# Separate rings for the B rows and the C rows of a selective scan, and dt's bias written into delta's buffer

## The reference, cut to what matters

```python
dlt, Bm, Cm = jnp.split(u @ W_x.T, [64, 80], axis=-1)      # 64 ranks, 16 B rows, 16 C rows
delta = jax.nn.softplus(dlt @ W_dt.T + b_dt)
A = -jnp.exp(A_log)                                        # 256 channels x 16 states
dA = jnp.exp(einsum('bld,dn->bldn', delta, A))
dBu = einsum('bld,bln,bld->bldn', delta, Bm, u)
# in chunks of 32 positions: carry = a * carry + bu ; y = sum over states of carry * C
y = y * silu(res);  out = y @ W_out.T + b_out
```

## Time and profile before

| | us |
|---|---|
| median of three runs | 1179.11 |
| lowest and highest run | 1177.35, 1183.39 |
| the profiled execution: its time | 1166.19 |
| the profiled execution: its span, first to last instruction | 1164.5 |
| busy in the span: PE, DVE, POOL, ACT | 1028.6, 785.3, 669.2, 650.5 |
| moved by DMA in the span | 176.69 MB |

### The profile page before, as it was taken

How to read it: one execution, slowest core, us unless ns; L and a number is a source line. 1 busy time by engine, 2 the same in 40 slices (tenths; PEclk the granted TensorE clock), 3 DMA queues, 4 the chain that set the end, 5 groups by cost and what they waited for, 6 DMA issues and landing times.

```text
span 1164.5 us, 12622 instructions
## 1 busy us (share of the span) xinstructions
PE 1028.6 (88%) x4164; PEld 556.4 (48%) x4164; DVE 785.3 (67%) x1564; ACT 650.5 (56%) x1021; POOL 669.2 (57%) x572
## 2 busy tenths in 40 slices
PE   5999999998999999779899998988997879776865
PEld 4986668553356455434445444533543324222441
DVE  3322415878667876887687777888789788878721
ACT  3235557576956768555556768466644644543211
POOL 2122236566766477656856567756856876865501
PEclk9989999999888999989899999889898999898976
DMA  4002003535444353555544434645464656566320
GB/s 117 10 1 82 1 27 131 216 144 187 137 160 164 110 208 110 179 201 182 217 154 160 176 120 170 242 164 204 160 250 161 233 203 242 197 207 242 109 82 10
DMA packets 55721, 176.69 MB, mean 152 GB/s; under 512 B 7332, under 2 KB 17896, under 8 KB 51560
## 3 DMA queue, kind: packets, MB, share of 16 engines
q1 hardware_dynamic: 55656, 175.89, 42.8%
HBM read 172.99 MB, written 2.88 MB: 151 GB/s over the span
## 4 chain that ended last, share of the span: by engine, by line
PE 50%; DVE 14%; POOL 13%; ACT 10%; issue 6%; DMA 4%; SPq 1%; POOLq 0%; DVEq 0%; ACTq 0%
PE yp L1464 11%; POOL dbu L654 5%; PE mp L1349 4%; PE mp L1339 4%; PE fp L1253 4%; PE fp L1247 4%; DMA bcast<-held 3%; PE fp L1232 3%; PE pp L1378 3%; DVE dA L949 3%; PE pp L1308 2%; PE pp L1313 2%; PE yp L1446 2%; ACT a_z L997 2%; ACT L980 2%
## 5 line engine op out<-in xcount | busy, mean ns | idle before, releaser
L654 POOL TENSOR_TENSOR dbu<-du,bcast 128x1024 f32<-128x1024 f32 x128 | 302.7, 2368 | 148.3 <-DMA bcast<-held 78.8
L1464 PE MATMUL yp<-hs,ident 128*128 128x512 f32 x512 | 276.3, 673 | 32.3 <-DVE hs L956 25.7
L949 DVE TENSOR_TENSOR_SCAN dA<-dA,dbu 128x512 f32<-128x512 f32 x192 | 226.3, 1215 | 66.1 <-ACT dA L1191 44.7
L1191 ACT ACTIVATE dA<-delta,mA 128x496 f32<-128x496 f32 x256 | 165.9, 669 | 133.0 <-DVE dA L959 101.6
L1464 PEld LDWEIGHTS yp<-hs,ident 128*128 128x128 f32 x512 | 103.2, 214 | 161.5 <-issue 109.3
L882 DVE SCALAR_TENSOR_TENSOR he<-mp,vectors,he 128x512 f32<-128x512 f32 x128 | 89.6, 742 | 50.7 <-PE mp L1339 35.9
L956 DVE TENSOR_TENSOR hs<-dA,bcast 128x1024 f32<-128x1024 f32 x96 | 117.5, 1224 | 4.2 <-PE yp L1464 1.1
L1339 PE MATMUL mp<-cont,w_e 64*128 64x512 f32 x256 | 92.3, 685 | 13.7 <-DVE he L882 12.1
L980 ACT ACT_TABLE_LOAD x76 | 97.5, 1283 | 1.4
L638 POOL TENSOR_TENSOR hs<-hs,bcast 128x1024 f32<-128x1024 f32 x32 | 77.1, 2409 | 33.9 <-DVE hs L949 33.7
L949 DVE TENSOR_TENSOR_SCAN hs<-dA,dbu 128x512 f32<-128x512 f32 x64 | 75.0, 1206 | 18.3 <-ACT dA L1191 17.4
(11 more groups left out here) (217 smaller groups left out, 1554.4 us busy)
## 6 DMA issues: line engine op xcount, KB each, us to landing
bcast<-held SPq DMA_DIRECT2D x128, 1024.0 KB, 5.5
he<-gates SPq DMA_DIRECT2D x32, 1024.0 KB, 7.9
xin<-L_attn_x SPq DMA_DIRECT2D x8, 256.0 KB, 4.4
out<-xo SPq DMA_DIRECT2D x8, 256.0 KB, 2.3
held<-bc SPq DMA_DIRECT2D x8, 64.0 KB, 2.1
he<-conv_wT SPq DMA_DIRECT2D x1, 384.0 KB
w<-w1T SPq DMA_DIRECT2D x1, 256.0 KB, 3.1
he<-w2T SPq DMA_DIRECT2D x1, 256.0 KB, 3.7
```

The costliest lines, as they stand in the source:

```text
L654: pool.tensor_tensor(out=dbu[:, j % 2, :].rearrange("p (r t) -> p r t", r=2), in0=d, in1=b_n, op=ALU.mult).then_inc(dbu_r.sem, 1)
L949: dve.tensor_tensor_scan(out=h, data0=dA[:, half], data1=dbu[:, j % 2, half], initial=0.0, op0=ALU.mult, op1=ALU.add).then_inc(hs_r.sem, 1)
L1191: act.activation(out=dst, in_=src, func=ACT.Exp, scale=mA[:, c, n:n + 1]).then_inc(dA_r.sem, 1)
L1464: last = pe.matmul(yp[:, :], lhsT=ident[:, :], rhs=hs[:, j % 2, r * SEQ:(r + 1) * SEQ], start=(k == 0 and r == 0), stop=(k == PAIRS - 1 an ...
```

## The change

1. `bcast` (three slots with B and C together, 24 KB in a partition) becomes `b_rows` with four slots and `c_rows` with three, 28 KB in a partition. Each has semaphores for its slots. SP has a thread for each (letters B and C), and issues two DMAs of 512 KB for a step where it issued one of 1 MB. A B slot waits only for the `dbu` of step j-4. A C slot waits only for the multiplication by C of step j-3. The multiplications by C now wait for their own rows.
2. ACT writes W_dt's product plus bias into `delta`'s buffer, and Abs and the last step of softplus read it there. The wait for POOL's gate work moves from this write to the next sequence's write of `res`.
3. `m_bin2`, a small tensor of the setup, lies in the experts' memory `he`.
4. The table `ORDER` is another on all five engines.

```diff
-SLOTS = 3
+B_SLOTS, C_SLOTS = 4, 3
...
-        dab, dtb = cv, res
+        dab = cv
...
-        bcast = sb("bcast", [P, SLOTS, 2, 2 * SEQ])
+        b_rows = sb("b_rows", [P, B_SLOTS, 2 * SEQ])
+        c_rows = sb("c_rows", [P, C_SLOTS, 2 * SEQ])
...
+        m_bin2 = he[0:2, 6, INNER:2 * INNER]
...
-                            if j >= SLOTS:
-                                sp.wait_ge(dbu_r.sem, j - SLOTS + 1)
-                                _, by_pool, by_dve = with_c(j - SLOTS)
-                                if by_pool:
-                                    sp.wait_ge(hc_pool, by_pool)
-                                sp.wait_ge(hc_dve, by_dve)
-                            src = held[i % 2, :, 2 * k:2 * k + 2, :].rearrange("(a s) r t -> a s (r t)", a=1)
-                            sp.dma_start(bcast[:, j % SLOTS, :, :], src.broadcast_to([P, 2, 2 * SEQ])
-                                         ).then_inc(bc_in[j % SLOTS], 16)
+                    for j in range(i * STEPS, (i + 1) * STEPS):
+                        yield True
+                        if j % STEPS == 0:
+                            sp.wait_ge(bc_out.sem, bc_out.at(i, 16))
+                        if j >= B_SLOTS:
+                            sp.wait_ge(dbu_r.sem, j - B_SLOTS + 1)
+                        sp.dma_start(b_rows[:, j % B_SLOTS, :], rows(i, 0, j % PAIRS)).then_inc(b_in[j % B_SLOTS], 16)
+
+            def spread_c():
+                for j in range(BATCH * STEPS):
+                    yield True
+                    if j % STEPS == 0:
+                        sp.wait_ge(bc_out.sem, bc_out.at(j // STEPS, 16))
+                    if j >= C_SLOTS:
+                        _, by_pool, by_dve = with_c(j - C_SLOTS)
+                        if by_pool:
+                            sp.wait_ge(hc_pool, by_pool)
+                        sp.wait_ge(hc_dve, by_dve)
+                    sp.dma_start(c_rows[:, j % C_SLOTS, :], rows(j // STEPS, 1, j % PAIRS)).then_inc(c_in[j % C_SLOTS], 16)
...
-                            pool.wait_ge(bc_in[j % SLOTS], 16 * (j // SLOTS + 1))
+                            pool.wait_ge(b_in[j % B_SLOTS], 16 * (j // B_SLOTS + 1))
...
-                                dve.tensor_tensor(out=hs[:, j % 2, :], in0=dA[:, :], in1=bcast[:, j % SLOTS, 1, :],
+                                dve.wait_ge(c_in[j % C_SLOTS], 16 * (j // C_SLOTS + 1))
+                                dve.tensor_tensor(out=hs[:, j % 2, :], in0=dA[:, :], in1=c_rows[:, j % C_SLOTS, :],
...
+                    if i >= 1 and c == 0:
+                        act.wait_ge(g4_r.sem, g4_r.at(i - 1, 1))
                     act.activation(out=res[:, c, :], in_=pp[:, :], func=ACT.Identity,
...
-                    if c == 0:
-                        act.wait_ge(g4_r.sem, g4_r.at(i, 1))
-                    act.activation(out=dtb[:, c, :], in_=pp[:, :], func=ACT.Identity,
+                    act.activation(out=delta[:, b, c, :], in_=pp[:, :], func=ACT.Identity,
...
     "SP":
-        "AGAGGBBBBABBBGBGGBBBBBBAGGGBBBBBBBBBBBGBGGBABBBGGGBBBBBBBBBDBABBGBGGBBBGBBBBBBBGGBBBBBGBGGBBDGABBBGG"
+        "AGAGGBCCCBBBBABBCBCBCCBBGCGBGCBCBCBGCGGBCBACCCBCBBBBCCBBCBCBCCBBCBCGBGGCCBBACBGCBCCCBBBBCBCGGBCBCBCB"
```

More of the change, by code:

```diff
@@ L42 @@
+        "CBBCDBCBCCBBGGGCBCBCCCDGGGD",
     "Pool":
[L43 to L46, removed]
+        "FFFFFFFFFAFAFFFFFBBAAFFFAFFAASSFSASFFSSSSSFFAFASSSBBSAFSAFSFSSSSASFAFSSSSFAFSSFSSASBABSSSFAFFASAFSFS"
@@ L47 @@
+        "SSSASSFASASFBFSBASSSSASSBFBAFFASSASFSAFSSSSSFAAFBFSBASSSBSFBSASSFSFASASASSSFSFSASSSSAFSAFSSBFSBASSAS"
+        "FSSFFSSBBSSAASASSFASSFSSBASBSSSFASASSSSBBSSAASSSASASSSSSASSASASBSBSASSSSSSSSABASBSSSSSASSASSSSABASSS"
+        "BSSSSSSSSSSSSSAABBBB",
     "DVE":
[L48 to L50 removed]
@@ L356, in build @@
         yg = sb("yg", [P, IC, SEQ])
-        bc_in = [sem(f"bc_in{k}") for k in range(SLOTS)]
+        b_in = [sem(f"b_in{k}") for k in range(B_SLOTS)]
+        c_in = [sem(f"c_in{k}") for k in range(C_SLOTS)]
         dA_r = signal("dA_r", 2 * STEPS)
@@ L426, in _ @@
             load(ld_mamba, m_edge[:, :], A["conv_wT"][0:2, :])
-            load(ld_mamba, m_bin2[:, :], row(A["L1_attn_b_in_row"][0:INNER]).broadcast_to([2, INNER]))
+            load(ld_mamba, m_bin2, row(A["L1_attn_b_in_row"][0:INNER]).broadcast_to([2, INNER]))
             load(ld_mamba, mw_x[:, :, :], A["mamba_W_xT"].rearrange("(c p) m -> p c m", p=P))
@@ L445, in spread @@
                     if i >= 2:
-                        for s in range(SLOTS):
-                            used = sum(j % SLOTS == s for j in range((i - 1) * STEPS))
-                            sp.wait_ge(bc_in[s], 16 * used)
+                        for arrived in (b_in, c_in):
+                            for s in range(len(arrived)):
+                                used = sum(j % len(arrived) == s for j in range((i - 1) * STEPS))
+                                sp.wait_ge(arrived[s], 16 * used)
@@ L467, in gating, with rows @@
+            def rows(i, which, k):
+                src = held[i % 2, which, 2 * k:2 * k + 2, :].rearrange("(a r) t -> a (r t)", a=1)
+                return src.broadcast_to([P, 2 * SEQ])
             def gating():
@@ L637, in times_c @@
                 h = hs[:, j % 2, :]
-                pool.tensor_tensor(out=h, in0=h, in1=bcast[:, j % SLOTS, 1, :], op=ALU.mult).then_inc(hc_pool, 1)
+                pool.wait_ge(c_in[j % C_SLOTS], 16 * (j // C_SLOTS + 1))
+                pool.tensor_tensor(out=h, in0=h, in1=c_rows[:, j % C_SLOTS, :], op=ALU.mult).then_inc(hc_pool, 1)
             def s_thread():
@@ L652, in s_thread @@
                             d = du[:, i % 2, c, :].rearrange("p (a t) -> p a t", a=1).broadcast_to([P, 2, SEQ])
-                            b_n = bcast[:, j % SLOTS, 0, :].rearrange("p (r t) -> p r t", r=2)
+                            b_n = b_rows[:, j % B_SLOTS, :].rearrange("p (r t) -> p r t", r=2)
                             pool.tensor_tensor(out=dbu[:, j % 2, :].rearrange("p (r t) -> p r t", r=2),
@@ L904, in before_scan @@
                 dve.wait_ge(mln_r.sem, mln_r.at(i, 1))
-                dve.scalar_tensor_tensor(out=delta[:, b, :, :], in0=dtb[:, :, :], scalar=0.0, in1=dab[:, :, :],
+                dve.scalar_tensor_tensor(out=delta[:, b, :, :], in0=delta[:, b, :, :], scalar=0.0, in1=dab[:, :, :],
                                          op0=ALU.max, op1=ALU.add).then_inc(delta_r.sem, 1)
@@ L1156, in before_scan @@
                 act.wait_ge(dtb_r.sem, dtb_r.at(i, IC))
-                ch.add(act.activation(out=dab[:, :, :], in_=dtb[:, :, :], func=ACT.Abs))
+                ch.add(act.activation(out=dab[:, :, :], in_=delta[:, b, :, :], func=ACT.Abs))
                 ch.wait()
```

59 lines of the change are left out of this document (28 added, 31 removed).

## The result

The changed kernel takes 1157.53 us as a median of four runs (1155.21 to 1160.93). The kernel before took 1181.25 us beside it (1177.35 to 1190.7). The ratio on record is 0.9873, 95% interval 0.9828 to 0.9919. A later set of six runs gave 0.9829 (0.9787 to 0.9871). So it is 1.3 to 1.7% faster; 1165 us had been forecast, a ratio of 0.988. The two medians of the first set stand 23.7 us apart, more than its ratio says. Those are four runs each; in the later sets, with over 20 runs of the kernel before, its median is 1175.3 to 1177.1 us, 18 to 20 us above the changed kernel's.

The account below looks back on a forecast made before the run. PE was taken to bound the scan before 880 us, a loop of waits through the copies after it. Gains of 12 + 3 + 1 less 2 made 14 us, so 1179.1 - 14 = 1165 us, range 1154 to 1173.

Parts of the forecast that it names:

- What bounds the late stretch: From 880 to 1100 us no engine is full; the path runs copy, `dbu`, scan, multiplication by C, next copy.
- B rows in four slots: 12 + 3 us: B copies issued about two steps earlier end POOL's copy waits: 12 us gained after 880 us, 3 before.
- rival A: Late stretch: the wait moves to DVE's loop and nothing is won; gain 2 us, 1177 us; chance 0.20.
- The order: -2 us: PE's last expert pieces move behind the scan: 2 us lost in the tail; moves at changes of sequence summed to nothing.
- C rows add no wait: C copies have until the multiplication three steps later, about 20 us at the mean step; costed at nothing.
- Twice as many copies: nothing: SP issues 128 more copies, 46 us, covered by its waits for the multiplications; costed at nothing.
- The landing of half a copy: Copies of 512 KB: 5.5 us taken for the later half, ends 0 and 7.9, all within the new lead.
- The bias: 1 us: Bias of dt written into delta's buffer no longer waits for POOL's gate work; 1 us gained of 0 to 4.7.
- B's mechanism: Rival: delta comes late at changes of sequence, the first scan waits for Ln through `dbu`; slower, 1187 us; chance 0.17.
- C's time: Rival: copies were on the path wherever the chain has them late; gain 28 us, 1151 us; chance 0.11.
- D: Rival: half copies hold the DMA engines as long as whole ones, 7.9 us a step; 1273 us; chance 0.02.
- The signs of being right: POOL's B-row wait under 10 us, DVE's late `dbu` wait near 5, scan 10 to 20 shorter, no C-row wait, copies off chain.

Follow-up runs that it names:

- e4: Kernel before, old order and ring, but from the fourth step on a copy brings only 64 of the 1024 elements of each row; ratio 0.9995.
- e12: Kernel before's order and bias of dt in res, with the separate rings of four B and three C slots; ratio 0.9960 to the kernel before.
- e11: Kernel before with its order and ring, only the bias of dt written into delta's buffer; ratio 0.9980.
- e1: Changed kernel's separate rings and bias of dt in delta's buffer, with the order of the kernel before; ratio 0.9926 to the kernel before.
- e13: The changed kernel run again, nothing changed; median 1157.20 us, ratio 0.9829 to the kernel before.
- e5: Changed kernel with copies of 64 of the 1024 elements of each row from a slot's second use on; median 1156.97 us, ratio 0.9825.
- e6: Changed kernel with three B slots and four C slots in place of four and three; ratio 1.0016 to the kernel before.
- e7: Changed kernel with three B slots and three C slots; ratio 1.0041 to the kernel before.
- e3: Changed kernel, but the B copy also waits for the multiplication by C of step j-3, so no early B; ratio 0.9993 to the kernel before.
- e2: Kernel before (one ring of three slots, whole copies, bias in res) with the changed kernel's order; ratio 1.0332 to the kernel before.
- e10: Kernel before's order, two copies for a step without early B, bias of dt in delta's buffer; ratio 0.9945 to the kernel before.
- e8: Changed kernel with the bias of dt written into res again; median 1164.55 us, ratio 0.9892 to the kernel before.

## Why the prediction came out right, and which terms were wrong

1. **What bounds the late stretch.** Right as a reading of the chain: the copies left it, and `dbu` with them. Wrong as a price list: in the old order e4 took more than half of the copy waits away and e12 nearly all, and the time fell by nothing that can be told (e4) and by 0.4% (e12).

2. **B rows in four slots: 12 + 3 us.** This is the term that was mis-sized. POOL's waits for copies did go, as I took them to (none in the changed kernel, 6.5 us in e12), but with the order held this brought 0.4% (e12), some 5 us, with an interval from 1 to 8. The sum had given it 15. One sentence that failed is "I take 4 us for all this" for what stands behind a waiting `dbu`: ScalarE's wait for POOL's layer norm steps did not move (71.0 us in e12, 70.5 before). The other is the 8.1 + 3 us of DVE's waits: they fell by 6.9, from 20.9 us over the whole span to 14.0 in e12, DVE's waits for exponentials stayed (44.7 before, 45.5 in e12), and the scan from first to last `dbu` is 2.0 us shorter in the one profiled execution, 8.0 us against e11's. POOL's waiting has moved from the copies to DVE's scans (68.4 before, 100.4 in e12), so for the most part it waited for copies in time that it had to spare. That is rival A, for the greater part, at work inside a right total.

3. **The order: -2 us.** Wrong in sign. From e1 (same rings, same bias, old order) to the changed kernel the ratio goes from 0.9926 to 0.9873 or 0.9829, so the order brings 0.5 to 1.0%, 6 to 11 us, about half of the gain. (The sets were not run side by side, and the first ratio's interval overlaps e1's. But no run of e1, 1164.96 to 1174.2 us, is as short as the longest of the changed kernel's ten, 1160.93.) It does so only with these rings: 1.0332 with the old one, 1.0041 with three slots each. I had priced the moves that I could see one by one and summed the rest to nothing; the 10 us of PE's work that left the stretch where PE is full were not among them. Of the two prices that I did work out, one held in its form: at the last change of sequence, where no exponentials stand behind Ln, DVE's scans pause from 1001.33 to 1009.07, 7.7 us (7.7 in e13 too), as the form of the earlier trace rows had said (7.9):

```profile
1000.11 1.22 DVE L972 TENSOR_TENSOR hs<-dA,c_rows 128x1024 f32<-128x1024 f32 x1
...
1009.07 2.35 DVE L964 TENSOR_TENSOR_SCAN dA<-dA,dbu 128x512 f32<-128x512 f32 x2 [3.38 <-POOL dbu L669]
```

   The other, 2 us for the tail, can't be told: what follows the last `dbu` takes 76.9 us in the changed kernel and 75.0 in e13, the same program, for 74.3 before and 75.5 in e1, which has the old order.

4. **C rows add no wait.** Right. No wait of DVE or POOL in the changed kernel is put down to a C row. One place looks like it, at 481.39 us, where DVE idles 3.63 us before a multiplication and the view names no releaser. DVE and PE in order of time:

```profile
475.45 2.31 DVE L964 TENSOR_TENSOR_SCAN dA<-dA,dbu 128x512 f32<-128x512 f32 x2
...
479.42 1.88 PE L1480 MATMUL yp<-hs,ident 128*128 128x512 f32 x4
...
481.39 1.23 DVE L972 TENSOR_TENSOR hs<-dA,c_rows 128x1024 f32<-128x1024 f32 x1 [3.63 <-issue]
```

   The multiplication also waits until PE has added up the state of two steps before, whose buffer it writes, and those sums end at 481.30. Its own C row was issued at 459.35 and had long landed. The same place in e5, with C rows that land in 2.8 us:

```profile
487.33 1.88 PE L1482 MATMUL yp<-hs,ident 128*128 128x512 f32 x4
...
489.31 1.23 DVE L974 TENSOR_TENSOR hs<-dA,c_rows 128x1024 f32<-128x1024 f32 x1 [3.62 <-issue]
```

5. **Twice as many copies: nothing.** Right. SP still waits hundreds of us for slots. But I missed what its order does to others: the queue is in order, and a B copy that waits holds the gates. With four B slots this is small; with three it eats the gain (e6, e7).

6. **The landing of half a copy.** I took 5.5 us for the later half. Measured: 4.1 and 4.9; in pairs 3.9 for the first, 5.4 for the second (e3). I left out what the first half gains by landing by itself. In e3 against e2 this was up to 3.3%, less what the bias gave; in the old order, e10 against e11, 0.35% with intervals that overlap.
   The Trainium skill's formula ("DMA: Bandwidth & Descriptors", section "Anatomy of one DMA") gave 3.2 us for half a MB, and is given there for DMAs that GpSimd issues, while SyncE issues these; the shortest landing here took 3.3 us, the medians are 4.1 and 4.9. Its rule to keep DMAs at 1 MiB or more (section "Bandwidth") is outweighed here by a reader that needs one half only.

7. **The bias: 1 us.** Too small in the new order: 0.2 to 0.6% (e8), where the wait for POOL's gate work is 15.1 us long. In the old order 0.2% (e11), not told from nothing.

8. **The rivals.** B's mechanism is in the trace (7.7 us at the last change) and was outweighed. C's time, 1151, lies below the measured one. D is refuted, landings did not grow.

9. **The signs of being right.** All that I had named came true: POOL's wait for B rows gone, DVE's late wait for `dbu` 6.1 us, the scan 18.0 us shorter, no wait for C rows, copies off the chain. Yet they hold with two terms wrong, since none of them can tell the rings from the order.

So the total was right by luck: a term too large (rings, 15 for about 5) and terms too small (order, -2 for 6 to 11; bias, 1 for 2 to 7, of which the part beyond 2 is already in the order's 6 to 11) cancelled, and the 14 us forecast are still a little under the 15 to 20 measured. The place was wrong too: I had put 12 of the 15 us of the rings after 880 us, and of the 18 us by which the scan is shorter 12.8 lie in the first four sequences. What stays open is by which moves the new order gains. Sequence by sequence, first `dbu` to first `dbu`, it loses 35 us in the third (151.2 for 116.6) and gains it back and more around it (121.6 for 135.0 in the second, 107.3 for 138.6 in the fourth), so work of the other threads has changed places with the scan. The table above says how much of PE's work went from the first half to the second; no experiment here took a single move alone.

No experiment points to a version that beats both kernels: by e5, faster copies bring nothing more, and no run that does all the work was better than the changed kernel.

## What to carry to other kernels

- A wait on the chain is worth no more than the loop beside it allows. Before pricing it, shorten it in place (short copies did it here in a few lines). 79 us of waiting for copies and 13% of the late chain were worth 0.4% with the order held.
- Where a view names no releaser, look up every semaphore that the instruction waits for before blaming one. Short copies showed here that the wait for a C row was none.
- An order written out by hand and the buffers it was made for are one change. Each alone was between 3.3% slower and 0.7% faster; together they gave 1.3 to 1.7%. Judge slots not only by their reader: a copy that waits on an in-order queue holds the copies behind it.
- If two readers take halves of one transfer, try a transfer for each, the urgent half first: the first half landed in 3.9 us here, the whole in 5.9.

## What the runs showed of the hardware that I had not expected

- A copy of 64 KB in 256 pieces of 256 bytes took 4.3 us to land as a median (e4), one of 32 KB in 128 such pieces 2.8 us (e5), one of 512 KB in 128 pieces of 4 KB 4.1 to 4.9. With 16 times fewer bytes in as many pieces the median landing fell by 1.2 us from 5.5, and by 1.3 to 2.1 us from 4.1 to 4.9: most of it does not depend on the bytes. Whether the number of pieces counts is open: the medians of e4 and e5 differ by 1.5 us, their shortest landings (2.8 and 2.7 us) hardly.
- The time of one program goes with the mean granted clock, but loosely: the kernel before had runs of 1170.4 us at 0.921 and 1187.7 at 0.906, and at 0.915 runs from 1170.0 to 1181.8. A single profiled execution can be on either side, and here the spans show 11 us of the 15 to 20.
